# Windowed attention on one core: probabilities transposed three pairs behind the scores

## What is computed

```
qkv = xw @ qkv_w.T + qkv_b            # xw: windows x 49 tokens x 192
q, k, v = (qkv[0] * hd ** (-0.5), qkv[1], qkv[2])     # 12 heads of 16
attn = jnp.einsum('bhnd,bhmd->bhnm', q, k) + bias[None] (+ mask)
attn = jax.nn.softmax(attn, axis=-1)
out = jnp.einsum('bhnm,bhmd->bhnd', attn, v) ... @ proj_w.T + proj_b
x = x + out
```

## Time and profile before

| | |
|---|---|
| median of 3 runs | 4781.35 us (4780.85 to 4781.38) |
| profiled execution, its time | 4778.66 us |
| profiled execution, its span | 4776.7 us |
| busy share of the span: PE, PEld, DVE, ACT, POOL | 94%, 80%, 83%, 50%, 50% |
| attention stage | from about 2500 us to the end |

### The profile page before, as it was taken

How to read it: one execution, slowest core, us unless ns; L and a number is a source line. 1 busy time by engine, 2 the same in 40 slices (tenths; PEclk the granted TensorE clock), 3 DMA queues, 4 the chain that set the end, 5 groups by cost and what they waited for, 6 DMA issues and landing times. The chain is left out here.

```text
span 4776.7 us, 123308 instructions
## 1 busy us (share of the span) xinstructions
PE 4503.8 (94%) x42504; PEld 3833.8 (80%) x42504; DVE 3946.8 (83%) x7850; ACT 2366.2 (50%) x4594; POOL 2379.3 (50%) x2098
## 2 busy tenths in 40 slices
PE   0599999999999999999969999999999999999998
PEld 0488888888888888888857888888888888888887
DVE  6788888888888888888827888888888888888887
ACT  0244444444444444444415555555555656555565
POOL 1245554555555554555425555555555555555555
PEclk9999999999999999999969999999999999999999
DMA  8011111111111111111112222222222222222222
GB/s 341 21 38 39 39 41 38 38 39 39 41 37 39 39 41 37 39 40 41 34 40 67 69 68 69 69 67 71 67 70 69 68 68 69 70 68 70 67 70 59
DMA packets 397987, 285.95 MB, mean 60 GB/s; under 512 B 155355, under 2 KB 396235, under 8 KB 396747
## 3 DMA queue, kind: packets, MB, share of 16 engines
q1 hardware_dynamic: 395204, 283.19, 20.2%
q10 hardware_dynamic: 2736, 2.14, 0.1%
HBM read 120.34 MB, written 87.31 MB: 43 GB/s over the span
## 5 line engine op out<-in xcount | busy, mean ns | idle before, releaser
L882 POOL TENSOR_TENSOR E<-E,ri 128x588 f32<-128x588 f32 x512 | 646.3, 1262 | 1028.5 <-DVE ri L1107 1028.3
L602 PE MATMUL ps_o<-w,g_hi 128*128 128x384 f32 x2352 | 710.9, 365 | 5.9 <-DVE g_lo L542 4.1
L414 ACT ACTIVATE gF<-ps_g,b1f 128x512 f32<-128x512 f32 x588 | 404.7, 688 | 393.0 <-PE ps_g L633 390.7
L960 ACT ACTIVATE E<-L 128x588 f32<-128x588 f32 x512 | 356.1, 695 | 475.6 <-POOL L L888 242.5
L1097 DVE SCALAR_TENSOR_TENSOR L<-ps_s,bias 128x588 f32<-128x588 f32 x512 | 394.5, 770 | 178.0 <-PE ps_s L1241 161.9
L602 PE MATMUL ps_o<-w,g_lo 128*128 128x192 f32 x2352 | 534.8, 254 | 0.0
L1249 PE MATMUL ps_t<-ident,E 128*98 128x128 f32 x3072 | 441.3, 280 | 41.1 <-POOL E L882 41.1
L441 POOL TENSOR_TENSOR res<-xt,b2b 128x768 f32<-128x768 f32 x98 | 181.5, 1852 | 591.1 <-DVE x L490 591.1
L400 ACT ACTIVATE h_hi<-ps_h,hbias 128x512 fp32r<-128x512 f32 x196 | 123.1, 679 | 703.7 <-PE ps_h L617 703.7
L1249 PEld LDWEIGHTS ps_t<-ident,E 128*98 128x98 f32 x3072 | 313.4, 127 | 195.4 <-POOL E L882 108.3
L1241 PE MATMUL ps_s<-Kp,Q 64*64 64x196 f32 x6144 | 455.4, 342 | 2.7 <-DMA Kp<-K 2.7
(11 more groups left out here) (211 smaller groups left out, 12090.5 us busy)
## 6 DMA issues: line engine op xcount, KB each, us to landing
xs<-in_x SPq DMA_DIRECT2D x8, 4704.0 KB, 22.0
xt<-in_x SPq DMA_DIRECT2D x98, 384.0 KB, 3.4
x_cells<-x SPq DMA_DIRECT2D x784, 48.0 KB
xb<-x_cells SPq DMA_DIRECT2D x128, 294.0 KB
Vx<-V SPq DMA_DIRECT2D x512, 73.5 KB
out<-yo SPq DMA_DIRECT2D x128, 294.0 KB
Kp<-K SPq DMA_DIRECT2D x512, 49.0 KB, 1.9
Kp<-K SPq DMA_DIRECT2D x512, 24.5 KB, 1.8
```

Of the source, the lines that this page charges most:

```text
L414: act.activation(gF[f % 4][:, :], ps_g[:, f % 2, :], ACT.Gelu, bias=b1f[:, f:f + 1]).then_inc(s_gelu, 1)
L602: last = pe.matmul(dst, g[:, f, P * k:P * (k + 1)], w, start=(f == 0 and i == 0), stop=(f == FT - 1 and i == 1))
L882: pool.tensor_tensor(e, e, ri[p][:, :].unsqueeze(2).to_broadcast([P, HEADS, T]), ALU.mult)\
L960: act.activation(E[pp][:, :, :], L[pp][:, :, :], ACT.Exp).then_inc(s_ex, 1)
```

## The change

The transposes and PV of a pair move one place further back: three pairs behind the scores (`LAG = 3`) and no longer two. With it the order of each engine's slot is rewritten:

- PE: both halves of `turn` now stand behind the transposes at p = 0 and ahead of PV, `mix` 0 moves from p = 0 to p = 2, `project` 1 moves behind PV at p = 1, `project` 2 and `values` 0 behind PV at p = 2.
- DVE: the subtraction stands directly behind the maxima; sums and reciprocals of the pair before move behind it and behind `lower` and `queries_b`; `finish` 0 moves from p = 0 to p = 2.
- POOL: `less_max` of pair p stands ahead of `norm` of pair p - 1.
- ACT: the PT copy stands ahead of the exponentials, `upper` 0 and 1 follow each other, the copy of the queries goes to the end of p = 2.
- The three PSUM banks are used in another order, and the waits that guard them move along.

No instruction is added to a unit and none is taken away.

```
-            OUT0, TURN, QK, VAL, OUT1 = 0, 1, 3, 6, 8
+            LAG = 3
+            TURN, KEYS, OUT0, QRY, VAL, OUT1 = 0, 2, 4, 5, 6, 8
...
-                return (u, c, p - 2) if p >= 2 else (u - 1, 1 - c, p + 2)
+                return (u, c, p - LAG) if p >= LAG else (u - 1, 1 - c, p + UP - LAG)
...                                                     # POOL
+                        if is_unit(u):
+                            less_max(u, p)
                         if is_unit(pu):
                             norm(pu, pp)
-                        if is_unit(u):
-                            less_max(u, p)
...                                                     # DVE
-                        if is_unit(pu):
-
-                            dve.wait_ge(s_ex, k)
-                            dve.tensor_reduce(sm[pp][:, :], E[pp][:, :, :], AX.X, ALU.add).then_inc(s_sm, 1)
-                            dve.wait_ge(s_sm, k)
-                            dve.reciprocal(ri[pp][:, :], sm[pp][:, :]).then_inc(s_ri, 1)
                         if is_unit(u):
                             dve.wait_ge(s_mx, k + 1)
                             l = L[p][:, 0:HS, :]
                             dve.tensor_tensor(l, l, mx[p][:, 0:HS].unsqueeze(2).to_broadcast([P, HS, T]),
                                               ALU.subtract).then_inc(s_sub, 1)
-                        if is_unit(u - 1) and p == 0:
-                            finish(i, c, 0)
                         if nxt and p == 0:
                             lower(i, c, 0)
                             lower(i, c, 1)
                         if nxt and p == 1:
                             queries_b(i, c)
+                        if is_unit(pu):
+
+                            dve.wait_ge(s_ex, k)
+                            dve.tensor_reduce(sm[pp][:, :], E[pp][:, :, :], AX.X, ALU.add).then_inc(s_sm, 1)
+                            dve.wait_ge(s_sm, k)
+                            dve.reciprocal(ri[pp][:, :], sm[pp][:, :]).then_inc(s_ri, 1)
+                        if is_unit(u - 1) and p == 2:
+                            finish(i, c, 0)
...                                                     # PE
-                        if is_unit(u - 1) and p == 0:
+                        if is_unit(u - 1) and p == 2:
                             mix(i, c, 0)
                         if nxt:
+                            if p == 0:
+                                pe.wait_ge(s_xb[1 - c], 16 * LOADS * (i + c + 1))
+                                for h in range(2):
+                                    upto(pe, s_vc[h], v)
+                                turn(i, c, 0)
+                                turn(i, c, 1)
                             if p == 1:
                                 project(i, c, 0)
-                            if p == 2:
-                                project(i, c, 2)
                             if p == 3:
                                 values(i, c, 1)
-                        if nxt and p == 0:
-                            turn(i, c, 0)
-                        if nxt and p == 1:
-                            project(i, c, 1)
-                        if nxt and p == 2:
-                            values(i, c, 0)
                         if is_unit(lu):
...                                                     # waits, then PV
-                        if nxt and p == 0:
-                            turn(i, c, 1)
+                        if nxt:
+                            if p == 1:
+                                project(i, c, 1)
+                            if p == 2:
+                                project(i, c, 2)
+                                values(i, c, 0)
```

More of the change, by code:

```diff
@@ L734, in ps_w, with ps_qk @@
                 return banks[task % 3]
+            def ps_qk(step):
+                return ps_w(QRY if step == 2 else KEYS + step)
             ps_m, ps_b, ps_e, ps_q = banks[0], ps_s, banks[1], banks[2]
@@ L991, in slot @@
                             last.then_inc(s_o, 1)
-                        if nxt and p == 0:
-                            upper(i, c, 1)
+                        if nxt and p == 2:
+                            evacuated(i, c, 2)
                 units(act, slot)
@@ L1101, in slot @@
                             dve.tensor_reduce(mx[p][:, :], L[p][:, :, :], AX.X, ALU.max).then_inc(s_mx, 1)
+                        if is_unit(u):
+                            dve.wait_ge(s_mx, k + 1)
+                            l = L[p][:, 0:HS, :]
+                            dve.tensor_tensor(l, l, mx[p][:, 0:HS].unsqueeze(2).to_broadcast([P, HS, T]),
+                                              ALU.subtract).then_inc(s_sub, 1)
+                        if nxt and p == 0:
+                            lower(i, c, 0)
+                            lower(i, c, 1)
+                        if nxt and p == 1:
+                            queries_b(i, c)
                         if is_unit(pu):
@@ L1168, in turn @@
                 def turn(i, c, h):
[L1171 to L1178 removed]
+                    d, rows = 1 - c, CB if h else P
                     for p in range(UP):
@@ L1188, in project @@
                         pe.wait_ge(s_xl, 2 * v + 2)
-                        upto(pe, s_yo, 2 * (v - 2) + 1)
+                        upto(pe, s_yo, 2 * (v - 2))
+                    if step == 2:
+                        pe.wait_ge(s_qkm, 3 * v + 1)
+                        pe.wait_ge(s_qb, v + 1)
                     terms = W_QKV.terms(x_hi, x_lo, slice(P * m, P * (m + 1)))
                     for k, (w, x) in enumerate(terms):
-                        last = pe.matmul(ps_w(QK + step)[:, 0:UW], w, x, start=(k == 0), stop=(k == len(terms) - 1))
+                        last = pe.matmul(ps_qk(step)[:, 0:UW], w, x, start=(k == 0), stop=(k == len(terms) - 1))
                     last.then_inc(s_qk, 1)
@@ L1196, in values @@
                     v = 2 * i + c + 1
-                    pe.wait_ge(s_qkm, 3 * v + half + 1)
                     if half == 0:
-                        pe.wait_ge(s_qb, v + 1)
+                        pe.wait_ge(s_qkm, 3 * v + 2)
+                    else:
+                        upto(pe, s_yo, 2 * (v - 2) + 1)
                     for a in range(2):
@@ L1211, in mix @@
                     pe.wait_ge(s_o, UP * v + 2 * half + 2)
-                    if not is_unit(v + 2):
-                        pe.wait_ge(s_vc[0], UNITS)
+                    if is_unit(v + 2):
+                        if half == 0:
+                            pe.wait_ge(s_xl, 2 * (v + 2) + 2)
+                        else:
+                            pe.wait_ge(s_qkm, 3 * (v + 2) + 3)
+                    else:
+                        pe.wait_ge(s_vc[1], UNITS)
+                        pe.wait_ge(s_qkm, 3 * UNITS)
                         pe.wait_ge(s_yo, 2 * v)
-                    elif half == 0:
-                        pe.wait_ge(s_vc[0], v + 2)
-                    else:
-                        pe.wait_ge(s_qkm, 3 * (v + 2) + 3)
                     for a in range(2):
@@ L1244, in slot @@
                         if is_unit(lu):
-                            k = UP * u + p - 2
                             pe.wait_ge(s_nm, k + 1)
```

67 lines of the change are left out of this document (22 added, 45 removed).

## The result

The changed kernel takes 4968.42 us (median of 4 runs, 4968.02 to 4968.71) against 4781.36 us for the kernel before, measured beside it (4 runs, 4780.85 to 4782.25). The ratio is 1.0391, with a 95% interval of 1.0379 to 1.0403: 187 us slower. The forecast was 4959 us.

The account below looks back on a forecast made before the run. PE sets the pace: 16.90 us of work plus waits of 0.27, 0.39, 0.73, 0.77 and 0.06 make 19.12 us a unit against 17.67. The 1.45 more, taken as 1.4, times 127 adds 178 us: 4959, range 4840 to 5020.

Parts of the forecast that it names:

- The transposes' wait of 0.39 goes: PE's transposes no longer wait for POOL's norm: 0.39 us a unit, 50 us in all.
- PV p = 0 waits 0.27 for the PT copy: PE at p = 0: PV due at 2.29 starts at 2.56, as `mix` 0 no longer covers the gap.
- PV p = 1 waits 0.73 for the logits: PE at p = 1: PV waits 0.73 us for DVE's logits, with sums now behind `lower`.
- PV p = 2 waits 0.77: PE at p = 2: PV waits 0.77 us for logits, late because DVE's subtraction stands until POOL's `rs` is through.
- PV p = 3 waits 0.06: PE at p = 3: PV, due after `values` 1 at 16.98, waits 0.06 us for the PT copy.
- Keys by DMA cost nothing: Keys' spread for `mix` 1 ends by 15.9, `mix` 1 due at 17.65: margin 1.8 us, costed at nothing.
- Rival 1: DVE and POOL don't disturb each other here: no 0.77 wait, 18.35 us a unit, 4868 us; chance 0.16.
- Rival 2: POOL takes the turn twice, `less_max` going behind `rs` ahead of waiting DVE: +80 us, 5039 us; chance 0.08.
- Rival 3: Only the waits swap, logits ready at both PVs: 17.62 us a unit, 4775 us; chance 0.05.
- rival 4: DVE runs ahead, `lower` 0 starting by 3.2 and subtraction not held: 17.23 us a unit, 4725 us; chance 0.06.
- Rival 5: Transposes don't count for TensorE's clock, which falls to 1.2 GHz early in each unit: above 5400 us; chance 0.02.
- I use 1.4: Last step of the sum: 1.45 us more a unit taken as 1.4, times 127 units, 178 us.

Follow-up runs that it names:

- experiment 6: Changed kernel with `rs` ahead of `norm` on POOL, PE's logits waits moved behind PV, and both `upper` ahead of ACT's exponentials at p = 0: 4774.84 us.
- experiment 4: Changed kernel with `rs` ahead of `norm` on POOL and PE's waits for the logits moved behind PV at p = 1 and 2: 4824.74 us.
- experiments 1: Changed kernel with `rs` moved ahead of `norm` in POOL's order: 4890.2 us.
- experiment 2: Changed kernel with `rs` replaced by a two-column sum and memsets that keep POOL busy about as long, residual missing from the output: 4894.5 us.
- experiment 3: Changed kernel with PE's wait for the logits moved from PV to the last matmul of `project` 1 (p = 1) and to `values` 0 (p = 2): 4865.39 us.
- experiment 8: Changed kernel with DVE's sums and reciprocals put back ahead of the subtraction: 4918.26 us.

## Why the prediction was right

The walk of the unit against the timeline, both from the first scores (t = 3005.77 in the trace of after):

| | predicted | measured |
|---|---|---|
| PV p = 0 | 2.56 | 2.55 |
| `project` 0 | 4.99 | 4.95 |
| logits p = 1 start | 5.81 | 5.80 |
| PV p = 1 | 6.71 | 6.59 |
| subtraction p = 1 | 7.43 to 9.34 | 7.37 to 9.25 |
| scores p = 2 | 8.31 | 8.30 |
| logits p = 2 start | 10.91 | 11.01 |
| PV p = 2 | 11.81 | 11.83 |
| scores p = 3 | 14.48 | 14.43 |
| PV p = 3 | 17.04 | 17.16 |
| next unit | 19.12 | 19.24 |

- **The transposes' wait of 0.39 goes.** Right: one wait in ten units is left.
- **PV p = 0 waits 0.27 for the PT copy.** Measured 0.26 (due at 3006.59 + 0.61 + 0.86 = 3008.06, started at 3008.32). The row calls the idle time "issue", but ACT's timeline has the copy from 3007.56 to 3008.22, and PV follows 0.10 behind it, as the walk took it.
- **`project` 0 waits 0.39 for `lower` 1.** Measured 0.36 (3009.75 + 0.61 to 3010.72), and experiment 6 gains 0.36 a unit by removing it.
- **PV p = 1 waits 0.73 for the logits.** Measured 0.65; experiment 4 gains 0.53 by moving the wait.
- **PV p = 2 waits 0.77, because DVE stands behind `rs`.** Measured 0.71; experiments 1 and 2 take it away with 0.62 and 0.61 a unit, once by moving `rs` and once by making it a write.
- **PV p = 3 waits 0.06.** Measured 0.22 (the values' last step ends by 3022.71, PV starts at 3022.93). It was not the PT copy: that had ended at 3022.58 in ACT's timeline. In the next unit there is no wait (values from 3040.87, 1.07 of them, PV at 3041.95). Between 3000 and 3200 us every second unit has the 0.22 and the others at most 0.02, and that is the alternation of long and short units. The releaser isn't in the profile, and the cause stays open.
- **Keys by DMA cost nothing.** Right in the changed kernel, but the margin of 1.8 us was measured to the end of SP's issuing, and the data land later. In the changed kernel SP ends issuing at 3021.26 (3016.28 + 4.98) and `mix` 1 starts at 3023.57, 2.3 us on; in experiment 3 `mix` 1 waits and starts 1.33 us on. So the true margin was about 1.0 us.
- **Rivals.** Rival 1 (no disturbance) would have left the subtraction at 0.4; it took 1.88. Rival 2 (`less_max` goes ahead of the waiting DVE) would have ended the subtraction behind `less_max`; it ended at 3015.02 and `less_max` at 3015.56, which took 0.90 where it takes 0.68 alone, so it was POOL that gave way. Rival 3 needed logits in time, rival 4 an earlier `lower` and a free subtraction; neither came by itself. Experiment 4 makes rival 3's waits by hand and has 17.99 us where the rival's sum was 17.62; experiment 6 makes rival 4's and has 17.63 for 17.23. Both sums are about 0.4 too low, by the small gaps. Rival 5: the clock stayed at 1.00.

The term that was mis-sized is the last step of the sum: "I use 1.4". It rounded down 1.45 because each hand-off had been taken whole, and the 1.45 stood against the one unit of 17.67 us and not the mean of 17.61. In the mean a unit grew by 1.53 (19.14 less 17.61) and the spans differ by 189.9 us (4966.6 less 4776.7). The walk without rounding, against the mean unit, gives 19.12 less 17.61, 1.51 x 127 = 192. The hand-offs are whole after all.

That the sum comes this close is in part luck. The five waits were forecast at 2.22 us and measured at 2.20, because 0.18 too much in four of them meets 0.16 too little in the last. PE's work of 16.90 counts the transposes at 0.61, where the earlier trace rows also has 0.70 ahead of `mix` 0 (5.44 to 6.14); such gaps were put at nothing, and make the missing 0.14 of this unit (19.24 less 16.90 and 2.20). In the mean unit, where every second one lacks the 0.22, the two nearly cancel: 19.14 us against the walk's 19.12. One reading was wrong without harm: the norm that ends by 12.33 is that of pair 1, not of pair 0. And the prediction looked only for norms beside the subtraction; `less_max` stands beside nearly every one, which cost DVE nothing (last section).

The Trainium skill's page "TensorE: Matmul & The Clock Gate", Part 4, was the ground of rival 5, that transposes don't count for the clock. Here four pairs' transposes and both turns stand in each unit and the clock stays 1.00, with waits of 2.3 us a unit between them. The rows don't bear that rule out as a danger for this mix; whether it holds for transposes alone no run here shows.

In the experiments my forecasts for 3 and 4 were too low by 70 and about 30 us. In 3 the step that failed was to take the keys' transfer as hidden, by the same margin that was 0.8 us too wide. In both, a wait was booked as gain in full, where small gaps stay; the 12 and 16 us by which 1 and 2 came out above their forecasts, and the 33 of experiment 8, fit the same omission.

## What to carry to other kernels

A longer lag buys off a wait only where the work it moves away was covering nothing else: walk one unit with all engines' orders, and list what each instruction that waits is due for next. Where POOL has a long elementwise job on SBUF data, look at which two-input DVE instruction will start under it, and put that job where DVE has a PSUM input, one input or nothing to do (in experiment 4 `lower` and the sums ran under `rs` in their usual 0.62 and 0.77 us). Put a wait that guards a buffer at the last instruction before that buffer's reuse, and then look at what the shorter unit runs into.

## What the runs showed of the hardware that I had not expected

- A waiting DVE gets in between two POOL instructions that are queued: the subtraction had waited since 3013.14, `rs` ended at 3014.70, and POOL's next instruction, due at once, took 0.90 us where it takes 0.68 alone. The DVE one ended first.
- When both start together, DVE loses nothing and POOL does. After the change each subtraction starts with `less_max`, because both wait for the maxima. The whole span of the changed kernel:

```profile
L1107 DVE TENSOR_TENSOR L<-L,mx x512: 465/466/1909, 2516.3 to 4952.1; 128x294 f32<-128x294 f32 x171
L892 POOL TENSOR_TENSOR L<-L,mx x512: 895/958/962, 2516.3 to 4952.2; 128x294 f32<-128x294 f32 x171
L886 POOL TENSOR_TENSOR E<-E,ri x512: 1172/1174/1180, 2521.8 to 4956.6; 128x588 f32<-128x588 f32 x171
```

  `less_max` has 0.958 where 0.674 was the median before. The norm gained: 1.174, and 1.262 was usual while the subtraction ran into its start. `less_max` grew by 0.28 us, less than the 0.47 of the subtraction beside it. The subtraction's own 0.466 in place of 0.401 isn't the clash, for it is 0.47 in experiment 2 as well, beside memsets alone. It goes with the place directly behind the maxima that it needs: in experiment 8, with sums and reciprocals between the two again, it is 0.401, and in the kernel before the very first pair, which has no sums to make, has 0.47 (at 2515.72, right behind the maxima at 2514.92).
- PE has short gaps where nothing is late by the walk, for instance 0.08 us between the transposes and the first `turn` (due at 3007.20, started at 3007.28) and 0.22 ahead of PV at p = 3. The weight loads of the transposes have 41 such waits in 200 us, 11.7 us in all, with "issue" as their cause. They are in the kernel before too, and no run here took them apart.
